# A graph network kernel on one NeuronCore: nine one-hots a round on VectorE, the tenth on ScalarE, and no loads for empty batches

## The reference, cut to what matters

```python
x = LN(x + (1 + eps) * x + segment_sum(relu(x[src] + edge_attr), dst))
# two rounds of y = segment_sum(w * y[dst], src), w = dinv[src] * dinv[dst]
x = LN(x + two_rounds(x))
h = relu(segment_sum(x[src], dst) @ w_rel1 + x @ w_root1 + b1)
x = LN(x + segment_sum(h[src], dst) @ w_rel2 + h @ w_root2 + b2)
x = LN(x + relu(segment_sum(edge_weight * x[src], dst) @ w3 + b3))
```

## Time and profile before

| | |
|---|---|
| median of 3 runs | 8374.77 us (8360.94 to 8383.45) |
| the profiled execution: time, span | 8406.03 us, 8404.3 us |
| busy share of the span: PE, DVE, ACT, POOL | 78%, 83%, 55%, 62% |
| one-hots, L1051 on DVE | 2220 instructions, 1549.4 us |
| matmuls of the plain sums, L985 on PE | 14800 instructions, 1260.7 us |
| additions to the blocks, L551 on POOL | 2220 instructions, 1149.8 us |
| DMA | 1881.23 MB, mean 224 GB/s |

### The profile page before, as it was taken

The page is one execution under the profiler, slowest core; times in us unless marked ns, Lnnn a source line. Parts: engine busy times, 40 slices in busy tenths (PEclk is TensorE's granted clock), DMA queues, the critical chain, the costliest instruction groups (busy, mean ns, idle before and its releaser), DMA issues. The chain is left out here.

```text
span 8404.3 us, 217866 instructions
## 1 busy us (share of the span) xinstructions
PE 6553.4 (78%) x65965; PEld 5251.7 (62%) x65965; DVE 7010.6 (83%) x11424; ACT 4614.2 (55%) x13918; POOL 5211.7 (62%) x6131
## 2 busy tenths in 40 slices
PE   8999998999966668996668676857787768677777
PEld 6666666666655557994457445744576557666666
DVE  7666666667657889999989998999896989799996
ACT  0166666666656775446960695069506960499900
POOL 0177777777765555334765676557764765388853
PEclk9955555555555555556889888978897789655597
DMA  9577888773338884445869786968695869355395
GB/s 362 100 212 213 218 214 212 210 209 93 92 109 282 283 268 138 122 122 174 293 212 356 263 294 218 355 226 292 219 356 186 293 211 355 138 200 203 118 338 194
DMA packets 1102458, 1881.23 MB, mean 224 GB/s; under 512 B 440329, under 2 KB 618690, under 8 KB 1101610
## 3 DMA queue, kind: packets, MB, share of 16 engines
q1 hardware_dynamic: 774326, 1166.49, 45.7%
q0 software_dynamic: 224928, 446.16, 14.7%
q10 hardware_dynamic: 102612, 261.44, 9.5%
HBM read 1162.29 MB, written 928.60 MB: 249 GB/s over the span
## 5 line engine op out<-in xcount | busy, mean ns | idle before, releaser
L526 POOL DMA_INDIRECT messages_in_parts<-WORK,goal x1850 | 2017.6, 1091 | 719.5 <-issue 433.1
L502 POOL DMA_INDIRECT edge_rows<-WORK x1664 | 1603.1, 963 | 869.9 <-issue 469.3
L957 PE MATMUL psum<-BIG,WORK 128*128 x11840 | 1298.9, 263 | 688.2 <-DVE WORK L1255 373.7
L1255 DVE TENSOR_TENSOR WORK<-WORK,psum 128x1024 bf16<-128x1024 uint8 x1480 | 1705.7, 1217 | 137.0 <-PE psum L957 89.0
L711 ACT CAST WORK<-psum 128x432 bf16<-128x432 f32 (+1 forms) x4440 | 1728.3, 601 | 148.7 <-DMA messages_in_parts<-WORK,goal 116.9
L551 POOL TENSOR_TENSOR BIG<-BIG,WORK 128x48 f32 x2220 | 1149.8, 518 | 1029.0 <-DVE WORK L1321 396.3
L957 PEld LDWEIGHTS psum<-BIG,WORK 128*128 128x128 bf16 x11840 | 914.2, 113 | 1072.8 <-issue 967.1
L1051 DVE TENSOR_TENSOR WORK<-lane_k,slot_part 128x1024 bf16<-128x1024 bf16 x2220 | 1549.4, 730 | 17.4 <-PE psum L957 17.4
L985 PE MATMUL psum<-WORK 128*128 128x144 bf16 x14800 | 1260.7, 235 | 358.6 <-DVE WORK L1051 269.8
L985 PEld LDWEIGHTS psum<-WORK 128*128 128x128 bf16 x14800 | 1099.4, 147 | 520.0 <-issue 383.7
L963 PE MATMUL psum<-BIG,WORK 128*128 x17760 | 931.0, 213 | 335.5 <-DVE WORK L1257 293.8
(11 more groups left out here) (184 smaller groups left out, 9844.4 us busy)
## 6 DMA issues: line engine op xcount, KB each, us to landing
WORK<-messages_in_parts SPq DMA_DIRECT2D x1850, 288.0 KB, 4.5
WORK<-parts_by_slot SPq DMA_DIRECT2D x444, 640.0 KB
messages_in_parts<-BIG ACTq DMA_DIRECT2D x37, 2880.0 KB
WORK<-blocks_by_edge SPq DMA_DIRECT2D x416, 256.0 KB
edge_rows<-BIG ACTq DMA_DIRECT2D x1, 76960.0 KB, 221.4
BIG<-edge_rows SPq DMA_DIRECT2D x74, 1040.0 KB
BIG<-whole_messages SPq DMA_DIRECT2D x370, 193.5 KB, 2.4
whole_messages<-BIG ACTq DMA_DIRECT2D x37, 1920.0 KB
```

The costliest lines, as they stand in the source:

```text
L502: pool.indirect_dma_start(rows_dram, bass.IndirectOffsetOnAxis(ap=at_stage[g][:, j:j + 1], axis=0), row_buf[g][:, j, :], None).then_inc(s_ ...
L526: pool.indirect_dma_start(unit_dram, bass.IndirectOffsetOnAxis(ap=goal[1 - d][:, t:t + 1], axis=0), msg[c].rearrange("p k f -> p (k f)"), ...
L957: m = pe.matmul(o, select[c % GB][:, k, :], V3[:, ds(b * W3, W3)], start=True, stop=True)
L1255: m = v.tensor_tensor(SEL[c % GB], part_of_batch, here_p.to_broadcast([128, T * K]), ALU.is_equal)
```

## The change

In the five plain sum stages:
- Of each round of ten batches nine are *front* batches (numbers 9i to 9i+8 of round i, from 0 to 332), and the last, at ring place 9, is the *back* batch 333+i (`in_round`). For this input all 37 back batches and the front batches from 294 on are empty.
- DVE makes the nine front one-hots, into ten buffers of their own that lie over SEL and `part_row` (`front_onehot`); a one-hot waits only for the batch ten before it. Its reduction of a pair now comes two places later in its queue (behind odd n the pair n-5, n-4).
- ACT makes the back one-hot, laid out with the slot outermost (k, m): a copy of the 8 slot numbers to float32, eight activations |part - lane| of 128 x 128, then relu(1 - d) over all 1024. It starts once the last round's back batch is summed; there is one such buffer.
- The table stage also finds which batches are used (`batch_used`), with one more matmul and two more DVE steps per order. SP reads ten flags into registers each round and issues each message load under the condition that its batch is used; a skipped load still counts its semaphore, and the buffer keeps its old content, which is multiplied by a one-hot of zeros.
- POOL reads block numbers twice a round, nine and one, where it read eight each eighth batch.
- SP's loads of the next pass's first part tables wait until the whole sum stage is done, as their space now holds one-hots.

In the edge pass nothing changes but the semaphore's count. The core of the diff:

```diff
@@ constants and tiles
+FRONT = 9
+BACK_AT = (9,)
+BACK = len(BACK_AT)
...
+        back_part = [carve(P, [BACK, K]) for _ in range(2)]
...
+        onehot_of = [WORK[:, c * T * K // 2:(c + 1) * T * K // 2].bitcast(BF16).rearrange("p (m k) -> p m k", k=K)
+                     for c in range(RING)]
+        back_onehot = WORK[:, BACK_AT[0] * T * K // 2:(BACK_AT[0] + 1) * T * K // 2].bitcast(BF16).rearrange("p (k m) -> p k m", k=K)
...
+        def front_of(c):
+
+            return c - sum(b < c for b in BACK_AT)
+
+        def in_round(i, c):
+
+            return PAIRS * FRONT + i * BACK + BACK_AT.index(c) if c in BACK_AT else i * FRONT + front_of(c)
@@ SP, message loads and part tables
                 def load_messages(i):
+                    if kind != "edge":
+                        sp.load(used_regs[0:FRONT], batch_used[d][0:1, ds(in_round(i, 0), FRONT)])
+                        sp.load(used_regs[FRONT:RING], batch_used[d][0:1, ds(in_round(i, BACK_AT[0]), BACK)])
+                        is_used = [sp.snap(r, min_val=0, max_val=1) for r in used_regs]
                     for c in range(RING):
...
-                            sp.dma_start(msg[c].rearrange("p k f -> p (k f)").unsqueeze(1), unit_v[:, ds(i * RING + c, 1), :])\
-                                .then_inc(s_gath[c], 16)
+                            sp.dma_start(msg[c].rearrange("p k f -> p (k f)").unsqueeze(1), unit_v[:, ds(in_round(i, c), 1), :],
+                                         cond=is_used[FRONT + BACK_AT.index(c) if c in BACK_AT else front_of(c)]).then_inc(s_gath[c], 16)
...
                     wait_past(sp, s_sel, q * BATCHES)
+                    wait_past(sp, s_sum, q * BATCHES)
@@ POOL, additions
-                for t in range(BATCHES + LAG):
+                for i in range(PAIRS if kind != "edge" else 0):
+                    t, b = in_round(i, 0), in_round(i, BACK_AT[0])
+                    front_blocks = load_blocks(pool, sum_regs[0:FRONT], batch_block[d][0:1, t:t + FRONT])
+                    back_blocks = load_blocks(pool, sum_regs[FRONT:RING], batch_block[d][0:1, b:b + BACK])
+                    for c in range(RING):
+                        add_sum(i * RING + c, back_blocks[BACK_AT.index(c)] if c in BACK_AT else front_blocks[front_of(c)])
@@ ACT
+                def back_onehots(i):
+
+                    nth = (q - 1) * PAIRS + i
+                    t = in_round(i, BACK_AT[0])
+                    wait_past(act, s_back, (nth - 1) * BACK)
+                    act.copy(back_part[nth % 2], slot_part[d][:, t:t + BACK, :]).then_inc(s_lone, 1)
+                    act.wait_ge(s_lone, nth + 1)
+                    for j, c in enumerate(BACK_AT):
+                        if i > 0:
+                            act.wait_ge(s_sum, q * BATCHES + (i - 1) * RING + c + 1)
+                        for k in range(K):
+                            m = act.activation(back_onehot[:, k, :], lane_b[:, :], ACT.Abs,
+                                               bias=back_part[nth % 2][:, j, k:k + 1], scale=-1.0)
+                        m.then_inc(s_away, 1)
+                        act.wait_ge(s_away, nth * BACK + j + 1)
+                        act.activation(back_onehot, back_onehot, ACT.Relu, bias=ones[:, 0:1], scale=-1.0).then_inc(s_back, 1)
@@ PE
-                                m = pe.matmul(sum_bank(c), onehot[c % GB][:, :, k], msg[c][:, k, :], start=k == 0, stop=k == K - 1)
+                                m = pe.matmul(sum_bank(c), back_onehot[:, k, :] if c in BACK_AT else onehot_of[c][:, :, k], msg[c][:, k, :], start=k == 0, stop=k == K - 1)
@@ DVE, tables and sums
+                step(v.tensor_scalar(chosen[:, :], batch_no[:, :], stop[:, 0:1], None, ALU.is_ge))
+                product()
+                step(v.tensor_scalar(batch_used[o][:, :], bank[7][0:1, 0:BATCHES], float(NB), None, ALU.is_lt))
...
+                def front_onehot(n, c):
+
+                    wait_past(dve, s_sum, n + (q * BATCHES - (RING - 1)))
+                    equal(onehot_of[c], lane_mk, slot_part[d][:, in_round(n // RING, c), :]).then_inc(s_oh, 1)
...
+                    for n in range(BATCHES + 4):
+                        if n < BATCHES and n % RING not in BACK_AT:
+                            front_onehot(n, n % RING)
+                        if n % 2 == 1 and n >= 5:
+                            reduce_pair(n - 5)
```

56 lines of the change are left out of this document (40 added, 16 removed).

## The result

The changed kernel takes 8687.87 us (median of 4 runs, 8666.35 to 8728.24) against 8379.11 us of the kernel before in the same session. The ratio is 1.0376, with a 95% interval of 1.0335 to 1.0417: it is slower by 3.8%, where 8323 us and a gain were forecast. The profiled execution took 8728.24 us.

The account below looks back on a forecast made before the run. VectorE's queue was taken to bound the sum stages. Per pass 25.2 - 8.7 - 4.0 - 1.1 = 11.4 us; five passes 57, less 5 for tables, 52 saved: 8323 us by the median, range 8252 to 8388.

Parts of the forecast that it names:

- Loads: SP's queue in the sum stages: flags and ten issues take 5.6 of 7.66 us a round, hidden; +1.1 us per pass.
- The rival that came true: SP's queue: conditional loads cost over 0.65 us, so loads come late; late one-hots or loads together had chance 0.05.
- POOL's register loads: POOL's queue in the sum stages: one takes 0.566 us; two a round were taken as hidden, at no cost.
- the backlog: POOL's additions lagging VectorE in a sum stage: one more each round, about eight fit, full after some eight rounds.
- the rival with three lost places: POOL loses one place for the missing boundary and one per register load each round: 57 us longer, 8432; chance 0.12.
- POOL's missing place: Sum stages: nine boundaries behind one-hots for ten POOL additions; 0.3 us a round for 29 of 37 rounds, 8.7 us.
- The first rival: Sum stages: POOL costs nothing, as an addition slips in beside a reduction; 115 us saved, 8259; chance 0.20.
- the forecast sum: Whole kernel: 11.4 us saved per pass, 57 in five passes, less 5 for tables: 52 us.
- 5 x (25.2 - 8.7): Five sum stages: 25.2 us per pass from 39 fewer VectorE one-hots, less 8.7 for POOL's lost places.
- the drain: End of each sum stage: ten POOL additions behind the last reduction's start, 4.0 us more per pass.
- Loads left out: Sum stages: 76 of 370 message loads fall away per pass, worth nothing by themselves.
- they keep the DMA from becoming the bound: Sum stages: nine loads per 7.66 us round need 347 GB/s, below today's 355, so leaving loads out protects the round.

## Why the prediction was wrong

**The step that failed is *Loads*:** "SP issues one in 0.33 us", and "two register loads per round on SP; 2 x 0.57 + 10 x 0.45 is 5.6 of 7.66 us, hidden". Both terms were mis-sized, and together they moved the bound. The 0.33 us of the earlier trace rows is how long the DMA instruction takes, not how far apart two of them stand. In the loop they are 0.67 us apart without a condition and 0.774 with one, as the register work between them counts too (the 0.45 fits the first ten loads of a stage, whose addresses are constants: they are some 0.47 apart): the condition lengthens its FUSED_REGOPS from 0.046 to 0.151 us. The register load of nine was priced by that of eight in the earlier trace rows, at 0.57, and took 1.87. The sum is 10.34 us in three rounds of four and 9.2 in the fourth, not 5.6, and it is compared with 7.66. The trace of before held the first half: there SP had 1.3 us a round to spare (7.0 of 8.3; its waits for TensorE in 140 us are 20.6), and a look at its queue's start times, as I took it for VectorE, would have told so.

**The rival that came true was named and priced at 0.05**: "a conditional load cost SP over 0.65 us against 0.33 to 0.45". It cost 0.774. I gave that case no time of its own, so it weighed nothing in the range. An issue queue that gets work ought to be one of the worked-out rivals.

**POOL's register loads** "I take it as hidden in the backlog's waits". Wrong too, and by the same misreading: 2.06 + 0.29 us in three rounds of four. With SP out of the way that cost 125.6 us. It is what the rival with three lost places described (decided "beyond 1.6 us"), and it came about by the size of one load.

**POOL's missing place** was right in mechanism and in the price of a place. With both faults mended, rounds of pass 1 were 7.5 to 7.7 up to the fifth (up to the eighth was forecast), then 8.0 (7.9 to 8.0), and the wait was 0.32 us (0.3). One more boundary took that wait away. The first rival, that POOL costs nothing, is refuted. The gain was not the forecast one. The profiled execution lies 52 us below the one before, which is the forecast sum, but that is luck: the profiled execution of the kernel before was a long one of its kind (8406 against a median of 8375). By the ratio it is 24 us, with an interval of 2 to 46. In the stages 57 us were gained, where 5 x (25.2 - 8.7) is 82.5: the backlog was full sooner, and the rounds behind it average 8.07, not 7.96, with POOL's pauses.

**The other terms**: the drain 4.0 to 4.7 us (4.0); ScalarE 3.8 us (4.5 at most), and no wait of TensorE ends with it; two one-hots still take 1.29 us beside ScalarE; the gain in a round appears in the rounds of 7.5 without loads. The reading that a next addition starts when the one-hot is "already 0.1 us old" holds only behind a reduction; inside a pair it is 0.42 by the earlier trace rows, and nothing hangs on it. **Loads left out** "are worth nothing by themselves" was right; "they keep the DMA from becoming the bound" was wrong, since 355 GB/s was what the rounds asked for, and the engines gave 380.

Open is why POOL's queue pauses once in four rounds, and why SP's own round is some 0.27 us longer in some passes than in others. That conditions and flags together cost more than their sum follows from SP's spare time: SP's own rounds add, and in the kernels that it bounds they are the rounds of the stage.

## What to carry to other kernels

Before an issuing queue gets conditions, flags or register reads, take its pace from start to start in the loop, and its spare time per round; a queue without a busy row can still be the next bound. It shows as waits for loads, DMA engines that are less busy than before, and an issuing queue that never waits. When VectorE loses instructions, look whether another engine lived on the boundaries between them: a split of one instruction can be cheaper than the wait. Skipping transfers was worth nothing here, where they were hidden, and the test for it was the dearest part of this change.

## What the runs showed of the hardware

The times of register loads fit a count of reads of about 0.2 us each. Where the load begins at a multiple of 16 bytes, a read takes four numbers and the rest is read singly; where it does not, every number is a read of its own. By this count one number is one read (0.27 on SP, 0.29 on POOL), eight aligned are two (0.566), nine or twelve aligned are three (0.745 on SP, 0.81 on POOL), ten aligned are four (1.03), and nine unaligned are nine (1.87 on SP, up to 2.08 on POOL). The flags read in the kernel before, ten a round, fit: ten begin at a multiple of 16 bytes in every other round, and take 0.966 and 2.09. The other rounds begin 8 bytes off, so eight of their ten numbers could be two aligned reads, and the 2.09 says that they are not. The Trainium skill (Runtime: NRT & Kernel Launch, "Instruction fetch mechanics") gives some 200 ns per register even in bulk; the unaligned load agrees (1.87 / 9 = 0.208 us), the aligned one does not (0.81 / 12 = 0.068 us). For these loads a table is best laid out in whole groups of four.

A DMA issue costs the SP queue 0.67 us in this loop with a wait and an address, 0.774 with a condition; a skipped one saves only what its DMA instruction is shorter, 0.07 to 0.08 us in place of 0.333.

A 128 x 48 addition on POOL takes 0.28 to 0.29 us when VectorE makes no one-hot beside it, 0.71 beside a whole one-hot of 1024 columns that it started 0.1 us into, and 0.45 beside one of 512. It gets out 0.1 to 0.2 us behind the end of the one-hot instruction, so a shorter instruction on VectorE gave it a place sooner.
